# Moving the next tiles' normalisation into the middle of a feed-forward group, and their transposes ahead of it

## What is computed

```python
x = x + attention(layernorm(x))              # 16 heads, causal
h = act_quant(layernorm(x)) @ weight_quant(w1).T   # 1024 -> 4096
h = silu(depthwise_conv1d(h, conv_w) + conv_b)     # 3 taps along the rows
x = x + act_quant(h) @ weight_quant(w2).T          # 4096 -> 1024
```

## Time and profile before

| | |
|---|---|
| median of 2 runs | 2213.47 us (2213.22 to 2213.73) |
| the profiled execution | 2211.79 us |
| its span on the slowest core (4) | 2209.9 us |
| spans of the 8 cores | 2200.1 to 2209.9 us |
| busy: PE, DVE, ACT, POOL | 50%, 44%, 37%, 17% of the span |
| mean granted TensorE clock, core 4 | 0.714 |

### The profile page before, as it was taken

How to read it: one execution, slowest core, us unless ns; L and a number is a source line. 1 busy time by engine, 2 the same in 40 slices (tenths; PEclk the granted TensorE clock), 3 DMA queues, 4 the chain that set the end, 5 groups by cost and what they waited for, 6 DMA issues and landing times.

```text
span 2209.9 us, 23728 instructions; the slowest of 8 cores (2200.1 to 2209.9 us)
## 1 busy us (share of the span) xinstructions
PE 1099.5 (50%) x6998; PEld 600.6 (27%) x7038; DVE 967.6 (44%) x1906; ACT 816.4 (37%) x894; POOL 373.6 (17%) x383
## 2 busy tenths in 40 slices
PE   0756684435544345551044374563745736557555
PEld 0322331112222222221032242432423323343322
DVE  1344434523245545554456545453364533535340
ACT  3100000858754446561142543514425144252511
POOL 0000000000000000000012522415215152243431
PEclk9977895555555566665567787786877868778777
DMA  7111001654423353334733331312313123132300
GB/s 231 58 38 39 19 20 56 229 180 170 165 86 115 115 174 116 112 121 164 237 97 104 96 96 57 117 47 98 102 47 117 46 95 105 58 125 66 96 19 19
DMA packets 108272, 224.02 MB, mean 101 GB/s; under 512 B 4593, under 2 KB 70258, under 8 KB 104050
## 3 DMA queue, kind: packets, MB, share of 16 engines
q1 hardware_dynamic: 94962, 172.18, 24.0%
q0 software_dynamic: 13184, 50.34, 6.9%
HBM read 188.94 MB, written 33.55 MB: 101 GB/s over the span
## 4 chain that ended last, share of the span: by engine, by line
DVE 31%; PE 23%; ACT 13%; DMA 11%; issue 10%; POOL 8%; DVEq 1%; SPq 0%; ACTq 0%; POOLq 0%
POOL hsil L75 8%; PE psQK L75 8%; PE psO L75 6%; DVE amx L75 5%; DMA wbuf<-w1t 4%; PE psPV L75 4%; DVE smalls L75 4%; DVE t1s L75 3%; ACT PT L75 3%; DVE cbuf L75 3%; DVE tmpc L75 3%; DMA wbuf<-w2t 3%; ACT hf L75 2%; ACT hq L75 2%; PE psM L75 2%
## 5 line engine op out<-in xcount | busy, mean ns | idle before, releaser
L75 PE MATMUL psM<-xqT,t1b 128*128 128x258 bf16 x2048 | 333.1, 333 | 341.5 <-DVE cbuf L75 332.4
L75 ACT ACTIVATE PT<-psS,smalls 128x1024 bf16<-128x1024 f32 (+1 forms) x320 | 315.5, 986 | 229.8 <-PE psS L75 200.3
L75 PEld LDWEIGHTS psM<-xqT,t1b 128*128 128x128 bf16 x2048 | 234.2, 118 | 442.9 <-issue 376.5
L75 PE MATMUL psS<-qT,kT 64*128 64x512 bf16 x640 | 173.3, 545 | 194.9 <-ACT PT L75 189.0
L75 DVE SCALAR_TENSOR_TENSOR tmpc<-psM,convw_s,tmpc 128x256 f32<-128x256 f32 x256 | 123.8, 483 | 316.8 <-ACT tmpc L75 222.9
L75 PE MATMUL psO<-t2T,hq 128*128 128x512 bf16 x1000 | 231.8, 393 | 40.8 <-ACT hq L75 38.8
L75 ACT ACTIVATE tmpc<-psM,convb_s,convw_s 128x256 f32<-128x256 f32 x256 | 144.5, 565 | 195.4 <-DVE cbuf L75 131.3
L75 POOL TENSOR_TENSOR hsil<-cbuf,hsil 128x1024 f32<-128x1024 f32 x64 | 150.4, 2349 | 301.8 <-ACT hsil L75 300.8
L75 POOL TENSOR_TENSOR hsil<-hsil,s2row 128x256 f32<-128x256 f32 x256 | 185.8, 726 | 57.2 <-DVE s2row L75 20.9
L75 ACT ACT_TABLE_LOAD x16 | 20.5, 1283 | 446.5 <-DVE smalls L75 324.6
L75 PE MATMUL psPV<-vaug,PT 128*128 128x65 bf16 x2176 | 112.9, 233 | 121.9 <-DVE PT L75 121.9
(11 more groups left out here) (79 smaller groups left out, 1105.1 us busy)
## 6 DMA issues: line engine op xcount, KB each, us to landing
t1b<-t1scr SPq DMA_DIRECT2D x64, 1024.0 KB, 5.4
wbuf<-w1t SPq DMA_DIRECT2D x32, 1024.0 KB, 6.2
wbuf<-w2t SPq DMA_DIRECT2D x32, 1024.0 KB, 6.0
xstage<-x POOLq DMA_DIRECT2D x16, 512.0 KB, 4.0
x1st<-x POOLq DMA_DIRECT2D x4, 2048.0 KB, 18.4
x1scr<-x1st POOLq DMA_DIRECT2D x4, 2048.0 KB, 11.1
t1scr<-t1s SPq DMA_DIRECT2D x16, 512.0 KB, 3.5
t2scr<-t1s SPq DMA_DIRECT2D x16, 512.0 KB, 3.3
```

The source lines that it names most:

```text
L75: inst = getattr(self.raw, name)(*a, **kw)
```

## The change

The calls of `emit_xq_tile` leave the end of the group. Tile 2g+5 is now emitted inside group_A(g) at the end of quad e = 2, and tile 2g+6 at the end of quad e = 5; in the order of every engine they stand after the quad's convolutions and ahead of its shift and sigmoid. The calls of `emit_xq_back` for tiles 2g+3 and 2g+4 move from behind group_A(g) to ahead of it. Number and kind of the instructions are otherwise unchanged.

```diff
                         if hh % 4 == 3:
+                            if e == 2 and 2 * g + 5 < NT:
+                                emit_xq_tile(2 * g + 5)
+                            if e == 5 and 2 * g + 6 < NT:
+                                emit_xq_tile(2 * g + 6)
                             if qg >= 0 and e % 2 == 0:
                                 emit_shift(qg, e // 2)
...
             for g in range(NGRP):
                 if g >= 1:
                     emit_Q_pool(g - 1)
+                for st in (2 * g + 3, 2 * g + 4):
+                    if st < NT:
+                        emit_xq_back(st)
                 emit_group_A(g)
...
-                for st in (2 * g + 3, 2 * g + 4):
-                    if st < NT:
-                        emit_xq_back(st)
                 if g >= 1:
                     emit_Cmm(g - 1, 0)
...
                 emit_Brest(g)
-                for st in (2 * g + 5, 2 * g + 6):
-                    if st < NT:
-                        emit_xq_tile(st)
                 if g >= 1:
                     emit_Cev(g - 1, 1, store=True)
```

## The result

The changed kernel takes 2252.65 us (median of 11 runs, 2247.17 to 2268.92) against 2213.77 us before (10 runs). The ratio of the means is 1.0139, 95% interval 1.0097 to 1.0180: slower by 31 us (21 to 40), where 46 us had been forecast. Four of the ten runs before took 2230.6 to 2244.4 us and the other six 2212.6 to 2213.8, so by the medians the step is 38.9 us. The time lies inside the stated range, the step from before within 2% either way.

What follows compares the result with a forecast made beforehand. Waits, not busy engines, were taken to bound the kernel. Fronts inside groups and the later start add 196.5 us, the boundary gives back 150.3: +46.2 on the 2209.9 us span, median 3.6 above, so 2260 us, range 2240 to 2295.

Steps and rivals of the forecast that it cites:

- What bounded the kernel: Feed-forward stage: waits, not busy engines; two fronts and two backs at the boundary cost 29.6 us a group.
- Backs moved: Group end: second matmuls follow the last shift, 10.1 us back in groups 1 to 5; DVE copies hidden in POOL wait.
- Fronts taken from the boundary: Group boundary: the whole 19.5 us of two fronts comes back where Cev stands ahead of POOL's work.
- Start: Start of the stage: first group waits for the backs of tiles 3 and 4, 4.4 us added.
- Length of a front and table: Inside groups, quads 2 and 5: each front costs its full 12.9 us plus 1.28 us for the sigmoid's table load.
- The wait for the load: Ahead of each front: DVE waits for x1t, 2.0 us at quad 5, taking the median load of 4.6 us.
- PE after idle time: Quad 6 of groups 1 to 4: matmuls slower after idling (6.58 us against 4.57), adding 0.6 us a group.
- The hidden front: Rival: in mid-group DVE parts run beside the passes, only 5.0 us a front exposed, 2122 us; chance 4%.
- The cheap front: Rival: loads land in 3.6 us and waits and hand-overs overlap, 2 us less a front, 2238 us; chance 10%.
- Slow PE: Rival: slow matmuls after each front and at second matmuls reach the path, 30 us more, 2290; chance 9%.
- dear table switches: Rival: a table switch within ACT's work costs twice its row, 29 us more, 2289; chance 3%.
- late loads: Rival: x1t loads meet the t1b loads, each front waits 5.8 us longer, 64 us more, 2324; chance 8%.

Runs made afterwards that it cites:

- e1_backs_only: Kernel before with only the backs moved ahead of the group, fronts left at the boundary ahead of Cev: 2174.05 us, ratio 0.9798 to before.
- e4_no_table_switch: Changed kernel with logarithm and exponential of tiles 5 to 15 replaced by sigmoids (rstd wrong), so no table switches in the groups: 2222.77 us, 1.0021 of before.
- e3_loads_early: Changed kernel with x1t loads of tiles 5 to 15 issued early from SP instead of from POOL between products: 2236.94 us, ratio 1.0078 to before.
- e8_behind_sigmoid: e3_loads_early with both fronts emitted behind the quad's shift and sigmoid instead of ahead of them: 2198.96 us, ratio 0.9916 to before.
- e5_front_at_quad1: e3_loads_early with the first front at the end of quad 1 instead of quad 2, ahead of DVE's wait for POOL: 2190.73 us, ratio 0.9859 to before.
- e6_fronts_in_waits: Against before: one front ahead of Cmm(g-1,0), one behind Cev(g-1,1); x1t loads from SP; backs at ends of quads 0 and 1: 2096.90 us, ratio 0.9443.
- e10_scalar_operands: e5_front_at_quad1 with seven one-column front operations turned into tensor_scalar, second column as per-partition scalar: 2184.44 us, ratio 0.9841 to before.

## Why the prediction was right

- **What bounded the kernel.** Right. The four distances between amx reductions gave the price of fronts and backs, and e1_backs_only has the one part alone: 10.4 us a group in groups 2 to 5 (10.1 forecast).
- **Backs moved.** Right, the cover included: with both copies at the boundary DVE's wait for POOL is still 13.25 us. Their move saves 10.5 us between the last shift and amx in after (15.1 against 25.7), 0.4 more than forecast. That counts only in group 1: for groups 2 to 5 the forecast gave back the whole 29.6 us, however it is split.
- **Fronts taken from the boundary.** Right: from amx to the restart of quad 2 it is 75.2 - 55.7 = 19.5 us less in group 2, as forecast.
- **Start.** Right: 4.5 us in e1_backs_only (4.4). With group 0 it is 37.1 (36.8).
- **Length of a front and table.** Right: 12.84 and 1.29 us in the rows above, and e4_no_table_switch confirms 2.5 us of tables a front.
- **The wait for the load.** This is the term that was mis-sized, in two ways. The first is an error of reading: I added the issue (0.54 us) to the time to landing, but that time is counted from the start of the issue, as the rows above show (issue at 1431.31, landing 3.61 us later at 1434.92, DVE goes on at 1435.08). That made each of the 11 waits about 0.4 us too long (0.54 less the 0.16 from landing to DVE's start). The second is the landing: I took the median of all x1t loads, 4.6 us, from bounds of 3.6 and 10.4. The chain of after, on its slowest core, shows 6.9 and 5.2 us in group 0 and 4.9 and 4.8 in group 1 (on the other cores there 3.5 to 4.9), but from group 2 on 3.5 to 4.4, as in these three:

```profile
1431.31 3.61 DMA x1t<-x1scr
...
1472.92 3.53 DMA x1t<-x1scr
...
1573.19 4.38 DMA x1t<-x1scr
```

  Over all cores the 11 landings have a mean of 4.1 us, 0.5 less than 4.6. Together the waits were forecast at about 26 us (2.0 us at six places, 2.7 at quad 2 of groups 1 to 5) and came to 16.1, some 10 us less; e3_loads_early, which removes them, gained 13.4. Before, the loads of two tiles were issued together and so landed later; now each goes alone. That this is the reason was not tried.
- **PE after idle time.** The 0.6 us in groups 1 to 4 did not come: the quad took 6.14 us in group 4, and the second matmuls came 0.14 us behind the shift there as in group 1. That is 2.4 us. The amx reduction came 15.2 to 15.5 us behind the last shift on every core, as in group 7.
- **The sum.** Loads 10, PE 2.4, groups 6 and 7 0.8 and group 1's second matmuls 0.4, with about 1 us that I can't assign, make the 14.5 us between the forecast of the stage (1097.7) and the measured 1083.2. All of them went the same way, so no errors cancelled; the range of 55 us was wide enough for them. The price of a front in the groups without other change is (142.3 - 110.1) / 2 = 16.1 us, against 17.2 forecast and the break-even of 13.0, so the sign was right with room to spare; the step of 2.1% came out as 1.4% by the means and 1.8% by the medians, mostly by the loads.
- **The rivals.** The hidden front is out for this order: DVE and ACT wait for each other all along it. A part of it came true in e8_behind_sigmoid, where only the order on ACT changed; that order I had not considered. The cheap front (22 us less, 2238) came nearest: from group 2 on its loads did land in 3.4 to 4.6 us, but no hand-over overlapped. Slow PE and dear table switches did not show, and late loads only in group 0, where DVE waited up to 5.3 us.

## What to carry to other kernels

Work that alternates between two in-order engines is poorly hidden by strewing it among work that alternates between the same two. Here a front cost its whole length, with a table switch there and back, and still 11.2 us where one of its halves could run beside a stretch of the other engine alone. It was hidden best where the engines wait for a third one; so look in the timeline for the longest waits on a third engine (here 12 us on POOL, 7 us on PE) and emit it there, and first of all behind whatever that third engine is waiting for. And when a step is moved, its DMA issue and what stands behind it on PE move with it: move them apart.

## What the runs showed of the hardware that I had not expected

A DVE operation on a single column, 0.16 us otherwise, took up to 2.81 us in e5_front_at_quad1 when it read two tensors from SBUF while POOL worked, and all 40 such operations over 1 us, on 8 cores, ended within 0.03 us of the end of POOL's product. Beside POOL's short multiplications (0.73 us each) the longest took 0.60 us in e6_fronts_in_waits and 0.73 us in the kernel before. With one tensor operand and a column as scalar none took over 0.22 us. The Trainium skill (SBUF — State Buffer, section SBUF: two separate sides) describes the two engines' shared port pair as an exclusive lock that is held for a whole instruction, also for DVE operations with two SBUF inputs; the trace agrees on the moment of release. It does not agree on who goes first: by the page the instruction that starts first gets the pair, but in 38 of the 40 cases DVE's operation starts 0.2 to 0.4 us ahead of the product, while POOL issues the load of x1g (1418.17 in the rows above), and waits all the same. No run here settles why. It also means that DVE time beside POOL is dearer: the fronts at quad 1 took 15.7 to 16.5 us instead of 12.84, and 13.2 to 13.6 us in e10_scalar_operands.
